# Graph stage of a four-layer kernel: both ELUs as relu plus residual with the second exponential clamped at one, and the tokens' normalisation moved to GpSimd between its gathers

## The reference, cut to what matters

```python
def _gat(inp, adj_mask, W, a):
    h = jnp.matmul(inp, W)
    ...
    att = jax.nn.softmax(e, axis=2)
    h_prime = jnp.einsum('bij,bjf->bif', att, h)
    return jax.nn.elu(h_prime)
out = jax.nn.relu(jnp.matmul(x, mlp1_w) + mlp1_b)
residual = out
out = _gat(jax.nn.relu(out), None, W_fc, a_fc)
out = jax.nn.elu(out) + residual
out = jax.nn.relu(jnp.matmul(out, mlp2_w) + mlp2_b)
residual = out
out = _gat(jax.nn.relu(out), adj, W_hand, a_hand)
out = jax.nn.elu(out) + residual
return jax.nn.relu(out)
```

## Time and profile before

| what | value |
|---|---|
| median of 3 runs | 1070.05 us (1064.08 to 1070.69) |
| span of the profiled execution | 1059.3 us |
| PE, DVE, ACT, POOL busy in the span | 88%, 68%, 62%, 48% |
| mean granted TensorE clock | 0.962 |

### The profile page before, as it was taken

The page is one execution under the profiler, slowest core; times in us unless marked ns, Lnnn a source line. Parts: engine busy times, 40 slices in busy tenths (PEclk is TensorE's granted clock), DMA queues, the critical chain, the costliest instruction groups (busy, mean ns, idle before and its releaser), DMA issues. The chain is left out here.

```text
span 1059.3 us, 25141 instructions
## 1 busy us (share of the span) xinstructions
PE 927.0 (88%) x8021; PEld 805.6 (76%) x8021; DVE 717.5 (68%) x2252; ACT 661.1 (62%) x1691; POOL 504.2 (48%) x498
## 2 busy tenths in 40 slices
PE   1799998999899999999998994798898888768997
PEld 1588887887688999999998993466565666548896
DVE  4599888988464135555554544579898888678775
ACT  4556665654544546666665662688888888867652
POOL 2566564663035564444444442576767732244340
PEclk9999998999699999999999996999999999978999
DMA  7913221211354216777676861011111100000112
GB/s 195 371 50 122 120 109 70 114 42 54 101 148 131 65 49 194 212 202 197 198 200 173 210 162 33 23 33 34 32 35 28 35 6 1 1 1 20 41 42 60
DMA packets 93007, 103.59 MB, mean 98 GB/s; under 512 B 16352, under 2 KB 69856, under 8 KB 90720
## 3 DMA queue, kind: packets, MB, share of 16 engines
q1 hardware_dynamic: 73232, 59.78, 17.3%
q10 hardware_dynamic: 11472, 25.63, 9.0%
q0 software_dynamic: 8192, 16.79, 5.5%
HBM read 52.60 MB, written 43.27 MB: 91 GB/s over the span
## 5 line engine op out<-in xcount | busy, mean ns | idle before, releaser
L1319 POOL DMA_INDIRECT slot_rows_in<-xn_all,slots x128 | 130.1, 1016 | 142.7 <-DMA slot_rows_in<-xn_all,slots 105.8
L1205 ACT ACTIVATE s_hT<-s_hp,expert 128x256 f32<-128x256 f32 x284 | 111.5, 476 | 52.4 <-PE s_hp L1196 52.4
L1218 PE MATMUL s_yp<-w_experts,s_hT 128*128 x1136 | 138.0, 275 | 0.0
L1218 PEld LDWEIGHTS s_yp<-w_experts,s_hT 128*128 128x128 f32 x1136 | 132.8, 192 | 0.0
L1226 DVE TENSOR_TENSOR xnT_all<-s_yp,expert 128x256 f32<-128x256 f32 x71 | 30.2, 425 | 117.9 <-PE s_yp L1218 114.7
L489 DVE SCALAR_TENSOR_TENSOR l_mi<-l_sbc,mT 128x512 bf16<-128x512 f32 x128 | 84.3, 668 | 4.0 <-PE l_sbc L480 3.3
L1194 PE MATMUL s_hp<-e_xh,e_wh 128*128 128x256 f32 x284 | 85.9, 303 | 0.0
L1196 PE MATMUL s_hp<-e_xh,e_wl 128*128 128x256 f32 x284 | 80.1, 282 | 0.0
L1195 PE MATMUL s_hp<-e_xl,e_wh 128*128 128x256 f32 x284 | 80.1, 282 | 0.0
L1176 ACT CAST e_wh<-expert 128x512 fp32r<-128x512 f32 x71 | 43.9, 619 | 48.8 <-issue 43.1
L1120 ACT ACTIVATE s_hT<-s_hp,b_shared 128x512 f32<-128x512 f32 x64 | 42.8, 688 | 48.4 <-PE s_hp L1091 47.2
(11 more groups left out here) (353 smaller groups left out, 2701.0 us busy)
## 6 DMA issues: line engine op xcount, KB each, us to landing
expert<-expert_rows ACTq DMA_DIRECT2D x65, 322.0 KB, 3.4
slot_rows_in<-zeros SPq DMA_DIRECT2D x9, 1024.0 KB, 12.2
xnT_all<-slot_rows_in SPq DMA_DIRECT2D x71, 128.0 KB, 3.4
slot_rows_out<-xnT_all SPq DMA_DIRECT2D x71, 128.0 KB, 2.8
slot_rows_out<-zeros SPq DMA_DIRECT2D x8, 1024.0 KB, 4.4
xn_all<-l_xr SPq DMA_DIRECT2D x16, 256.0 KB, 2.3
xnT_all<-l_rT SPq DMA_DIRECT2D x16, 256.0 KB
out_dram<-xn_all SPq DMA_DIRECT2D x16, 256.0 KB, 2.3
```

The lines of the kernel that those rows point to most:

```text
L1205: nc.scalar.activation(hT[q % 2][:, c, :], hp[:, c, 0:TILE], ACT.Gelu, bias=wt[q][:, F + c:F + c + 1]).then_inc(s["h_ok"], 1)
L1218: ins = pe.matmul(yp[q % 2][:, h * D:(h + 1) * D], hT[q % 2][:, c, h * P:(h + 1) * P], w2, start=(c == 0 and h == 0), stop=(c == FC - 1), ...
L1319: pool.indirect_dma_start(k.rows_in, bass.IndirectOffsetOnAxis(ap=k.slots[:, c, b:b + 1], axis=0), k.xn[:, b, :], None).then_inc(scattered ...
```

## The change

In the graph stage both ELUs are written in another form. With r the residual, the old form computes max(exp(min(exp(y), 1) - 1) - 1, y) + r. The new form computes min(exp(exp(y) - 1), 1) + (max(y, 0) + r), which is larger by exactly one. The clamp moves behind the second exponential, so ACT's second exponential needs nothing from DVE between the two, and the sum of relu and residual can be made beside it. In stage e the surplus of one is taken off in the last step: max(s2, 1) is added to x, where x was prepared as one less (the experts' biases are lowered by one at L1512). In stage c the surplus goes through the second weights, so their column sums are made in the experts' phase (two matmuls with one column) and subtracted from the bias.

The residual of stage c, which GpSimd added, is now part of a DVE step. In its place GpSimd takes over the normalisation of the tokens. It stands after the first two of the eight gathers of a slot; the other six follow it. That of group 0 stands after all eight gathers of group 4.

```diff
 def pe_table(pe):
     pe.transpose(counts[0:EC, 16:16 + J], last_of[:], k.ident[0:J, 0:J])
+    for c in range(2):
+        pe.matmul(counts[:, W2_SUM:W2_SUM + 1], k.w_mlp2[:, c, :], k.ones[:, 0:1], start=(c == 0),
+                  stop=(c == 1), skip_group_check=True)
...
-                dve.tensor_tensor(b2, b2, k.b2_shared[:].unsqueeze(1).to_broadcast([P, EXPERTS, D]), ALU.add)\
-                    .then_inc(s["table"], 1)
+                dve.scalar_tensor_tensor(b2, b2, -1.0, k.b2_shared[:].unsqueeze(1).to_broadcast([P, EXPERTS, D]),
+                                         ALU.add, ALU.add).then_inc(s["table"], 1)
+                dve.tensor_tensor(k.b_mlp2[:], k.b_mlp2[:], counts[:, W2_SUM:W2_SUM + 1], ALU.subtract)
...
-        def dve_n_apply(dve, g, p):
-            wait(dve, s["xT_ps"], g)
-            wait(dve, s["rstd_ok"], g + 1)
+        def pool_n_apply(pool, g, p):
+            wait(pool, s["xT_ps"], g)
+            wait(pool, s["rstd_ok"], g + 1)
             for b in range(GB):
-                ins = dve.tensor_scalar(xn[:, b:b + 1, :], batch(k.x, g, b), mv[p][:, b, 0:1],
+                ins = pool.tensor_scalar(xn[:, b:b + 1, :], batch(k.x, g, b), mv[p][:, b, 0:1],
                                         rstd[p][:, b:b + 1], ALU.subtract, ALU.mult)
...
         def pe_a_dense(pe, g):
-            wait(pe, s["t1_ok"], g - 1)
+            wait(pe, s["z1_ok"], g - 1)
...
         def act_a_r1(act, g, p):
-            wait(act, s["u1_ok"], g - 1)
+            wait(act, s["z1_ok"], g - 1)
...
-        def dve_c_cut(dve, g):
-            wait(dve, s["v1_ok"], g + 1)
-            dve.tensor_scalar(v1[:], v1[:], 1.0, None, ALU.min).then_inc(s["v1_cut"], 1)
-
         def act_c_exp2(act, g):
-            wait(act, s["t1_ok"], g)
-            wait(act, s["v1_cut"], g + 1)
+            wait(act, s["u1_ok"], g)
+            wait(act, s["v1_ok"], g + 1)
             nc.scalar.activation(w1[:], v1[:], ACT.Exp, bias=k.neg_one[:]).then_inc(s["w1_ok"], 1)
-        def dve_c_max(dve, g):
-            wait(dve, s["u1_ok"], g)
-            wait(dve, s["w1_ok"], g + 1)
-            dve.scalar_tensor_tensor(t1[:], w1[:], -1.0, mm[:], ALU.add, ALU.max).then_inc(s["t1_ok"], 1)
-        def pool_c_residual(pool, g, p):
-            wait(pool, s["r2_ps"], g)
-            wait(pool, s["t1_ok"], g + 1)
-            pool.tensor_tensor(u1[:], t1[:], r1T[p][:], ALU.add).then_inc(s["u1_ok"], 1)
+        def dve_c_linear(dve, g, p):
+            wait(dve, s["u1_ok"], g)
+            wait(dve, s["v1_ok"], g + 1)
+            dve.scalar_tensor_tensor(z1[:], mm[:], 0.0, r1T[p][:], ALU.max, ALU.add).then_inc(s["z1_ok"], 1)
+        def dve_c_sum(dve, g):
+            wait(dve, s["r2_ps"], g)
+            wait(dve, s["z1_ok"], g + 1)
+            wait(dve, s["w1_ok"], g + 1)
+            dve.scalar_tensor_tensor(u1[:], w1[:], 1.0, z1[:], ALU.min, ALU.add).then_inc(s["u1_ok"], 1)
...
-        def dve_e_cut(dve, g):
-            wait(dve, s["v2_ok"], g + 1)
-            dve.tensor_scalar(v2[:], v2[:], 1.0, None, ALU.min).then_inc(s["v2_cut"], 1)
         def act_e_exp2(act, g):
-            wait(act, s["t2_ok"], g)
-            wait(act, s["v2_cut"], g + 1)
+            wait(act, s["s2_ok"], g)
+            wait(act, s["v2_ok"], g + 1)
+        def dve_e_sum(dve, g):
+            wait(dve, s["s2_ok"], g)
+            wait(dve, s["q2_ok"], g + 1)
+            wait(dve, s["r2T_ps"], g + 1)
+            dve.scalar_tensor_tensor(z2[:], q2[:], 0.0, as_batches(rr[:]), ALU.max, ALU.add).then_inc(s["z2_ok"], 1)
         def dve_e_out(dve, g):
-            wait(dve, s["s2_ok"], g)
-            wait(dve, s["w2_ok"], g + 1)
-            dve.scalar_tensor_tensor(t2[:], w2[:], -1.0, q2[:], ALU.add, ALU.max).then_inc(s["t2_ok"], 1)
             wait(dve, s["x_ok"], g)
-            wait(dve, s["r2T_ps"], g + 1)
-            wait(dve, s["t2_ok"], g + 1)
-            dve.tensor_tensor(s2[:], t2[:], as_batches(rr[:]), ALU.add).then_inc(s["s2_ok"], 1)
+            wait(dve, s["z2_ok"], g + 1)
+            wait(dve, s["w2_ok"], g + 1)
+            dve.scalar_tensor_tensor(s2[:], w2[:], 1.0, z2[:], ALU.min, ALU.add).then_inc(s["s2_ok"], 1)
...
         def dve_slot(dve, g, half, p, on):
             if on["e"]:
-                dve_e_cut(dve, g - 1)
+                dve_e_sum(dve, g - 1)
...
             if on["c"]:
-                dve_c_cut(dve, g + 1)
+                dve_c_linear(dve, g + 1, q)
...
-            if on["a"]:
-                dve_n_apply(dve, g + 3, q)
             if on["c"]:
-                dve_c_max(dve, g + 1)
+                dve_c_sum(dve, g + 1)
...
                 pool_gather(pool, FIRST, range(8))
+                pool_n_apply(pool, 0, 0)
                 for g in range(-2, GROUPS):
...
                     if more:
-                        pool_gather(pool, g + FIRST + 2, range(0, 6))
+                        pool_gather(pool, g + FIRST + 2, range(0, 2))
+                    if on["a"]:
+                        pool_n_apply(pool, g + 3, (g + 3) % 2)
+                    if more:
+                        pool_gather(pool, g + FIRST + 2, range(2, 8))
                     if g == B:
                         last.pool_program(pool, (0,))
-                    if on["c"]:
-                        pool_c_residual(pool, g + 1, (g + 1) % 2)
-                    if more:
-                        pool_gather(pool, g + FIRST + 2, range(6, 8))
                     if on["b"]:
                         pool_b_scale(pool, g + 2)
```

More of the change, by code:

```diff
@@ L1038, in experts_phase @@
         READ_PREFIX = 16
+        W2_SUM = 80
         SPLIT = 2
@@ L1659, in pe_row @@
         if g == 0:
-            pe.wait_ge(graph["t1_ok"], GROUPS)
+            pe.wait_ge(graph["z1_ok"], GROUPS)
         wait(pe, s["rank_ok"], g)
@@ L1773, in pe_out @@
         if g < 2:
-            pe.wait_ge(graph[("q2_ok", "s2_ok")[g]], GROUPS)
+            pe.wait_ge(graph[("q2_ok", "z2_ok")[g]], GROUPS)
         wait(pe, s["out_ok"], g - 1)
@@ L1940, in graph_and_last_phase @@
         p1T = sb("p1T", [P, GB * P])
-        v1, w1, t1, u1 = (sb(n, [P, H1, GB * P]) for n in ("v1", "w1", "t1", "u1"))
+        v1, w1, z1, u1 = (sb(n, [P, H1, GB * P]) for n in ("v1", "w1", "z1", "u1"))
         r2T = [sb(f"r2T{p}", [P, GB * P]) for p in range(2)]
@@ L1947, in graph_and_last_phase @@
         p2T = sb("p2T", [P, GB * P])
-        q2, v2, w2, t2, s2 = (sb(n, G4) for n in ("q2", "v2", "w2", "t2", "s2"))
+        q2, v2, w2, z2, s2 = (sb(n, G4) for n in ("q2", "v2", "w2", "z2", "s2"))
         tb = ps("tb", [P, 512])
@@ L2128, in pe_b_sums @@
             wait(pe, s["r1_ok"], full(lambda n: n * H1, g, 1))
-            wait(pe, s["t1_ok"], g)
+            wait(pe, s["z1_ok"], g)
             wait(pe, s["p1T_ok"], g + 1)
@@ L2242, in pe_d_r2 @@
             wait(pe, s["r2_ok"], full(lambda n: n, g, 1))
-            wait(pe, s["s2_ok"], g)
+            wait(pe, s["z2_ok"], g)
             for b in range(GB):
@@ L2261, in dve_e_quotient @@
         def dve_e_quotient(dve, g, p):
-            wait(dve, s["t2_ok"], g)
+            wait(dve, s["v2_ok"], g)
+            wait(dve, s["z2_ok"], g)
             wait(dve, s["rden2_ok"], g + 1)
```

16 lines of the change are left out of this document (9 added, 7 removed), and 2 rows, old and new, of the table s.

## The result

| | before | after |
|---|---|---|
| median of the runs, us | 1069.01 (4 runs) | 1086.49 (4 runs, 1083.01 to 1098.60) |
| span of the profiled execution, us | 1059.3 | 1081.3 (its own time 1083.09) |
| mean granted clock of TensorE | 0.962 | 0.954 |

The ratio is 1.0188, with a 95% interval of 1.0137 to 1.0240. The forecast was 1068.2 us, range 1062 to 1076. The measured time is outside it, and the rival "POOL becomes the bound" came true, dearer than it was priced.

The account below looks back on a forecast made before the run. Bound: a chain across engines from POOL's scaling through PE, ACT and DVE. Terms + 5.1 + 0.4 - 1.0 - 3.45 - 0.8 - 1.65 - 0.4 = - 1.8 on 1059.3, plus 10.75: 1068.2 us, range 1062 to 1076.

Parts of the forecast that it names:

- POOL becomes the bound: Rival, chance 0.14: in slots that gather, POOL's own round of 17.2 us sets the period; 1076.8 us in all.
- POOL's slot: POOL's round in the graph stage: gathers, wait for 1/sigma, normalisations, scaling; priced at 15.2 us, so costing nothing.
- A: Time of the four token normalisations on POOL in one slot, taken as 1.6 us, with ends 1.1 and 2.2.
- 5.38: Time in us from the start of POOL's scaling until 1/sigma is ready, a term of POOL's round.
- The 7.9 us of the earlier trace: Time taken for the six gathers behind the normalisation on POOL, from a rested queue, a term of its round.
- The start: First group's normalisation stands behind eight gathers on POOL, so PE's first transpose comes later: + 5.1 us.
- the start is hidden: Rival, chance 0.12: the first slots wait for something else, so the 5.1 us shrink to nothing; 1063.1 us.
- The circle and its period of 16.46: Chain from POOL's scaling through PE, ACT and DVE sets each graph slot: 16.46 us, - 3.45 over slots 1 to 12.
- slot -1: Graph-stage slot where the leaky relu took 1700 ns beside POOL's residual; with the residual gone, - 1.0 us.
- slot 13: Graph-stage slot whose leaky relu shortens once POOL's residual is gone: - 0.8 us.
- the end: Slot 14, where PE no longer waits for POOL's residual, - 1.65 us, and slot 15 with the tail, - 0.4.
- 10.75 us: Time between profiled span and median of the runs, added to the new span of 1057.5 us.

Follow-up runs that it names:

- five: The changed kernel with a fifth normalisation instruction on POOL, repeating batch 3 into a buffer nobody reads; ratio to the kernel before 1.0348.
- two_wide: The changed kernel with POOL's four 128x128 normalisation instructions replaced by two of 128x512; ratio to the kernel before 0.9840.
- after_again: The changed kernel itself, run again on another chip; ratio to the kernel before 1.0145.
- start_early: The changed kernel with only the first group's normalisation moved, to between the fourth and fifth gather; ratio to the kernel before 1.0140.
- elu_early_again: The same kernel as elu_early, run on another chip; ratio to the kernel before 0.9939.
- wide_three: two_wide with three gathers instead of two ahead of the normalisation, and the first group's normalisation between the fourth and fifth gather; ratio to the kernel before 0.9946.
- elu_only: The changed kernel with the tokens' normalisation back on DVE, behind the linear part of stage c; ratio to the kernel before 0.9985.
- before_again: The kernel before, unchanged, profiled on another chip; period 16.2 to 16.8 us in four slots, 17.5 to 19.3 in the other six.
- elu_early: elu_only with the normalisation on DVE put ahead of the linear part of stage c; ratio to the kernel before 1.0040.
- elu_first: elu_early with the second layer's linear part also moved on DVE, behind the first layer's; ratio to the kernel before 0.9961.
- elu_early_third: The same kernel as elu_early, run a third time, in one set with wide_three_again; ratio to the kernel before 0.9977.
- immediates: The changed kernel with two constants for mean and 1/sigma in POOL's four instructions, so tokens are not normalised; one run, 1074.4 us.
- two_wide_again: The same kernel as two_wide, run in one set with after_again; ratio to the kernel before 0.9990.
- wide_three_again: The same kernel as wide_three, run in one set with elu_early_third; ratio to the kernel before 0.9749.

## Why the prediction was wrong

**The step that failed is POOL's slot**, priced at 13.6 + A = 15.2 us and measured at 18.9. Its worst term is A: "I take the two-input product of the same size on POOL, 404 ns, the nearest row: A = 1.6". The four take 3.14 to 3.3 us in most slots, 0.79 to 0.82 each, and 3.44 on the mean of slots 0 to 9. POOL's two rows, 404 and 558 ns, were of other forms, without two arithmetic steps and two operands of each partition. The rival's condition was "from A = 2.8", and the argument against it was that the small instruction "would have to take twice the nearest row". It takes twice the nearest row. five and two_wide show A in the period, up and down. The estimate from the Trainium skill (GPSIMD Engine Reference, section 3.1) was A = 1.4, and the rows show more than twice that; the measurement decides. It also counts 0.15 us of dispatch an instruction, a figure that this section of the Trainium skill gives for DVE and not for GpSimd.

**A alone does not make the loss.** With A = 3.3 and the rest as it was priced, the round is 16.9 us, 0.4 over the forecast's period. Over slots 0 to 9 of after, 1/sigma is used 6.63 us behind the scaling (5.38 in the sum), the four take 3.44 (1.6), gathers and hand-over 8.85 (8.2): 18.9, so 1.25 and 0.65 came on top of A's 1.84. The rival, with its A of 3.6, was too cheap by 1.7 us a slot for these two terms.

The gathers were mis-sized from the start. The 7.9 us of the earlier trace rows are the shortest of the eleven such trains in the trace of before; those of slots 0 to 9 there take 7.9 to 9.2, on the mean 8.4, and in after 8.3 to 9.2, on the mean 8.7. The train of slot 3 in before, of which these are the first and the last gather, takes 8.37:

```profile
735.49 0.99 POOL L1990 DMA_INDIRECT xn_all<-slot_rows_out,slots  x1
...
742.92 0.94 POOL L1990 DMA_INDIRECT xnT_all<-slot_rows_out,slots  x1 [0.46 <-DMA xnT_all<-slot_rows_out,slots]
```

The later 1/sigma goes with PE's clock. The 5.38 were taken from a trace in which the clock never falls in these slots. In the slots of after and after_again with the clock at 1.00 behind the scaling, the normalisation starts at 5.4 to 5.9; in those with the low stretch, in which h2 and the sums run slower, at 6.7 to 7.6. A slot of after_again with the clock at 1.00 throughout:

```profile
807.44 1.05 POOL L2115 TENSOR_TENSOR g_pn<-g_p,g_rden 128x512 f32<-128x512 f32 x1
...
813.00 3.29 POOL L2026 TENSOR_SCALAR g_xn<-x_tok,g_mv,g_rstd 128x128 f32<-128x128 f32 x4 [2.11 <-ACT g_rstd L2020]
...
825.11 1.06 POOL L2115 TENSOR_TENSOR g_pn<-g_p,g_rden 128x512 f32<-128x512 f32 x1
```

That is 5.56 + 3.29 + 8.82 = 17.67, and the six slots of after_again like it take 17.6 to 17.9. So A and the gathers make some 1.3 us over 16.46, and the rest up to 18.9 comes mostly with the low clock; one slot, slot 2 of after, is 19.08 without it, since its four normalisations take 4.67 (the "1.4 more" of the prediction, seen once). That POOL's lateness is what makes the clock fall is not shown: PE is busy for 1.36 of the 3 us around the scaling both in slots where it falls and in slots where it does not, and five, with a longer round, keeps 1.00 behind the scaling in six of its ten slots.

**The start** had the right mechanism and PE waited for exactly this instruction; 6.6 instead of 5.1 is A again, 3.15 for 1.6. The rival "the start is hidden" is out: start_early kept most of what it gained up to the first scaling.

**The circle and its period of 16.46** were right, though the change itself does not show it. elu_early_again has 16.45 or 16.46 in eight of ten slots, wide_three 16.45 to 16.52 in eight. What the prediction claimed of the ELU form holds in after as well: no wait of ACT's second exponentials on DVE, the leaky relu at 0.69 to 0.71, slot -1 -0.8 (forecast -1.0), slot 13 -1.1 (-0.8), the end -1.9 (-2.05), with the product right behind the transpose in slot 14 (955.17 and 956.05). What it did not see is that the ELU form alone is not free: its linear part is longer than the cut, so whatever stands behind it on DVE is late (elu_only, 17.4). In the change itself the normalisation had left DVE, so this cost nothing there.

**Time around the span.** The forecast added 10.75 us to the new span. The execution profiled after has 1.8 us around its span, before_again 1.9 (1072.98 and 1071.1); so the one profiled before was most likely a quick one of some 1061 us, an estimate from its span of 1059.3 and these 1.8. The difference of the medians is 17.5 us where that of the spans is 22.0. The 10.75 were then for the most part the distance between two executions, and not a part of one.

**The chances.** 0.14 for the rival was too low for what it rested on: a price that no row of the trace showed, with only 1.2 us between the value taken and the point from which it decides. Over 1080.8 us got 0.07, for a "still dearer instruction or a lost clock"; both came.

**What stays open.** On three of the chips, long slots came with waits that no recorded instruction ends. They were seen in every version that normalises on DVE there (before_again, elu_early, elu_first, elu_early_third) and in none of the versions that do it on POOL (two_wide, immediates, after_again, two_wide_again, start_early, wide_three_again), but before, elu_only and elu_early_again had none either on their chips. The recorded clock was at 1.00 when the one above began. The Trainium skill (TensorE: Matmul & The Clock Gate, section Seeing it yourself, the note on caveats of the trace) calls the recorded clock events unreliable; a low stretch that was not recorded would look like this, and no run here shows that it was one. wide_three's 0.975 may therefore mix a gain of its own with less of this loss in the versions beside it; how much of each was not tried. What decides whether the recorded clock falls behind the scaling is open as well.

## What to carry to other kernels

An engine that is off the circle has slack only against the whole round of its queue: add up what stands between the event that starts the round and the one that ends it, and put a number on the distance to the point where it takes over. If an added instruction is priced only from neighbours of another form, carry the upper end as twice the dearest of them, and give the rival a chance to match. Take such a term from all its rows and not from one: the train of gathers used here was the shortest of eleven. When an engine joins the circle, take the terms upstream of it anew and once more at TensorE's lower clock; and when work is moved on a queue, try the order (three gathers in front) and the width (two instructions for four) before the engine.

## What was unexpected of the hardware

- A GpSimd tensor_scalar of 128x128 fp32 with two operands per partition takes 0.79 to 0.80 us (shortest and median of 64), with two constants 0.67; a tensor_tensor of 128x512 with a broadcast takes 1.04 to 1.37, one of 128x128 0.40.
- A GpSimd instruction of 0.8 us took 2.28 when it started behind a two-input sum on DVE and a second such sum followed (five). The Trainium skill (SBUF — State Buffer, Who interferes with whom) has whole instructions exclude each other; by that rule the trace agrees.
- One kernel's median differed by 2.3% between chips (1059.6 to 1084.2 us), and one version's ratio to it by 1 to 2% (elu_early 0.994 to 1.004, wide_three 0.975 and 0.995). An interval of 0.4% on one chip does not carry over to the next.
- In the slots of after and after_again PE's granted clock fell to the lower level for some 3.4 us in twelve of twenty, and the normalisation started 1.4 us later on the mean in those (6.95 us behind the scaling, against 5.58).
